# Last slice of a weight product in three rounded passes, row products moved into the attention, staged waits, new step orders

## What is computed

```
q, k, v = h @ Wq + bq, h @ Wk + bk, h @ Wv + bv
a = q @ k.T / sqrt(512);  a = a * adj + (1 - adj) * (-1e6)
x = x + softmax(a) @ v
h = relu(layernorm(x))
agg = segment_sum(h[src], dst) / max(degree, 1)
x = x + h + alpha * (agg @ W.T + b)
```

## Time and profile before

| what | value |
|---|---|
| runs | median 236.33 us, lowest 236.18, highest 236.58 (3 runs) |
| the profiled execution | 236.24 us, of which span 234.4 us |
| PE busy | 230.7 us, 98% of the span |
| DVE busy | 161.5 us, 69% |
| ACT busy | 82.0 us, 35% |
| POOL busy | 73.3 us, 31% |
| granted TensorE clock | full (2.4 GHz level) in all 40 slices |

### The profile page before, as it was taken

One profiled execution on the slowest core, in us unless ns is written; L12 is line 12 of the kernel. 1 busy time (PEld: TensorE's weight loads), 2 busy tenths in 40 slices (PEclk: granted clock), 3 DMA queues, 4 the chain that ended last, 5 costly groups with the idle time before them and its releaser, 6 DMA issues.

```text
span 234.4 us, 3310 instructions
## 1 busy us (share of the span) xinstructions
PE 230.7 (98%) x1290; PEld 188.6 (80%) x1290; DVE 161.5 (69%) x282; ACT 82.0 (35%) x151; POOL 73.3 (31%) x106
## 2 busy tenths in 40 slices
PE   8999999999999999999999999999999999999995
PEld 6475888888888888888888888888888888888884
DVE  5999999998889855884749975757574262073222
ACT  3598906773142330431452442424242002060000
POOL 4277024410000059950702570706064206000000
PEclk9999999999999999999999999999999999999999
DMA  6999102000000030050000000000000000001232
GB/s 198 336 391 402 66 0 49 0 0 3 0 3 0 6 86 3 3 179 0 0 0 3 0 0 0 3 0 1 0 0 3 0 0 0 3 3 45 108 115 90
DMA packets 7153, 12.30 MB, mean 52 GB/s; under 512 B 1121, under 2 KB 2145, under 8 KB 7009
## 3 DMA queue, kind: packets, MB, share of 16 engines
q1 hardware_dynamic: 6272, 11.67, 14.3%
q10 hardware_dynamic: 864, 0.40, 0.6%
HBM read 9.97 MB, written 2.10 MB: 52 GB/s over the span
## 4 chain that ended last, share of the span: by engine, by line
PE 98%; DVE 0%; issue 0%; POOL 0%; DVEq 0%; POOLq 0%
PE bank L821 22%; PE bank L823 22%; PE bank L822 22%; PE bank L970 12%; PE bank L842 8%; PE bank L899 3%; PE bank L990 3%; PE bank L892 3%; PE bank L876 2%; PE bank L816 1%; PE bank L886 1%; DVE o_sb L803 0%; PE bank L849 0%; PE bank L865 0%; POOL ones_r L355 0%
## 5 line engine op out<-in xcount | busy, mean ns | idle before, releaser
L446 ACT ACTIVATE h2f<-xs,nmr,rstd 128x512 f32<-128x512 f32 x8 | 6.5, 816 | 56.1 <-POOL nmr L385 56.1
L821 PE MATMUL bank<-V_hi,pT_hi 128*128 128x512 f32 x64 | 25.5, 399 | 0.0
L577 DVE TENSOR_TENSOR ohW<-iotaW,key_b 128x1280 bf16<-128x1280 bf16 (+4 forms) x33 | 25.1, 761 | 0.0
L821 PE MATMUL bank<-hT_hi,GT_hi 128*128 128x512 f32 x64 | 25.1, 392 | 0.0
L823 PE MATMUL bank<-hT_hi,GT_lo 128*128 128x512 f32 x64 | 25.0, 390 | 0.0
L822 PE MATMUL bank<-V_lo,pT_hi 128*128 128x512 f32 x64 | 24.9, 390 | 0.0
L823 PE MATMUL bank<-V_hi,pT_lo 128*128 128x512 f32 x64 | 24.9, 390 | 0.0
L822 PE MATMUL bank<-hT_lo,GT_hi 128*128 128x512 f32 x64 | 24.9, 389 | 0.0
L970 PE MATMUL bank<-A,h_hi 128*128 128x512 f32 x64 | 24.9, 389 | 0.0
L970 PE MATMUL bank<-A,h_lo 128*128 128x512 f32 x64 | 24.9, 389 | 0.0
L573 DVE TENSOR_TENSOR ohL<-iotaL,lo_b 128x1024 bf16<-128x1024 bf16 x33 | 22.5, 683 | 1.5 <-PE bank L842 1.4
(11 more groups left out here) (133 smaller groups left out, 519.6 us busy)
## 6 DMA issues: line engine op xcount, KB each, us to landing
xs<-in_x SPq DMA_DIRECT2D x4, 512.0 KB, 8.4
out_dram<-o_sb SPq DMA_DIRECT2D x7, 256.0 KB, 2.0
wv_raw<-in_wv SPq DMA_DIRECT2D x1, 1024.0 KB, 11.6
wk_rows<-in_wk SPq DMA_DIRECT2D x1, 1024.0 KB, 12.6
wq_rows<-in_wq SPq DMA_DIRECT2D x1, 1024.0 KB, 11.4
wt_raw<-in_wT SPq DMA_DIRECT2D x1, 1024.0 KB, 5.2
wq_raw<-in_wqT SPq DMA_DIRECT2D x3, 256.0 KB, 8.0
wk_raw<-in_wkT SPq DMA_DIRECT2D x3, 256.0 KB, 8.2
```

The lines of the kernel that those rows point to most:

```text
L577: nc.vector.tensor_tensor(ohW[:, q % RING, :, 0:row].rearrange("p b (m two) -> p b m two", two=2), bcast(iotaW[:, 0:row].rearrange("p (m t ...
L821: mm(out, lhs[0][a], rhs[0][b], start=(first and k == 0), stop=False)
```

## The change

1. The slice k = 3 of M, four float32 products before, becomes rounded parts: ACT writes `w_high` of both weights (steps mh0, mh1), DVE the rests `wq_low`, `wk_low` (ml0, ml1), and M0 to M3 are three float32r matmuls each. Slice k = 2 becomes a step Mk2 of its own, in float32.
2. The eight products with u leave the first part. In the attention ACT normalises each block once more into two buffers (rows_once_more), and DVE multiplies them there: blocks 0 and 1 after its last projection step, then two in each of the rounds i = 0, 1, 2, behind the row maximum and ahead of pT_lo. POOL makes negc for each block by two small instructions ahead of its fill. u_sb now lies where the edge keys were, so it is loaded only after the last one-hot batch, and on SP's queue behind the wait for G7. The adding of bv is spread: four blocks after the first two fills, then two each in i = 1 and i = 2.
3. A product of G or V is issued term by term (four hi·hi, four hi·lo, four lo·hi) and waits for each operand ahead of its own term. The load of the last weight no longer waits for all of add_bv.
4. All four orders are new; G7 is now the last projection instead of V7.

```diff
-PE_ORDER = ("Mk0 Mk1 c3 bb M0 c2 M1 c2 T0 M2 T1 M3 T2 T3 c3 G0 G1 G2 G3 c1 V0 T4 c3 V1 T5 c3 T6 V2 V3 T7 c3 V4 V5 c3 G4 G5 "
-           "G6 c3 V6 c2 G7 c2 V7 c3")
+PE_ORDER = ("Mk0 Mk1 bb c3 Mk2 c2 T0 M0 T1 c2 M1 c1 M2 M3 T2 T3 c2 G0 G1 G2 G3 c3 V0 T4 c2 V1 T5 c3 V2 V3 c2 T6 V4 c3 V5 T7 "
+           "V6 G4 c3 G5 G6 c2 V7 c2 G7 c3")
...
+        u_sb = place("u_sb", [P, D], F32, r_e + 2 * 4 * ET)
...
-            sp.dma_start(u_sb[:, :], u_d.partition_broadcast(P)).then_inc(u_back, 16)
-
             sp.wait_ge(proj, proj_index(("G", NT - 1)) + 1)
             sp.dma_start(bv_sb[:, :], bv_d.partition_broadcast(P)).then_inc(ld_bv, 16)
+            sp.wait_ge(oh_ready, NB)
+            sp.dma_start(u_sb[:, :], u_d.partition_broadcast(P)).then_inc(u_back, 16)
...
             sp.wait_ge(counts_final, 1)
-            sp.wait_ge(res_ready, NT)
...
+                pool.wait_ge(dots, i + 1)
+                link(nc.gpsimd.tensor_scalar(negc[:, i:i + 1], c_f[:, i:i + 1], bb[:, :], -1.0, ALU.add, ALU.mult))
+                link(nc.gpsimd.tensor_scalar(negc[:, i:i + 1], negc[:, i:i + 1], NEG, None, ALU.add))
...
-            for t in range(NT):
+            for t in range(4):
                 add_bv(t)
...
+                if i <= 2:
+                    add_bv(2 * i + 2)
+                    add_bv(2 * i + 3)
...
+                elif step == "mh":
+                    k = SPLIT + n // 2
+                    act.wait_ge((ld_wq, ld_wk)[n % 2][k], 16)
+                    nc.scalar.activation(w_high[:, k - SPLIT, n % 2, :], (wq_raw, wk_raw)[n % 2][:, k, :], ACT.Copy).then_inc(m_hi, 1)
...
+            def rows_once_more(t):
+
+                if t >= 2:
+                    act.wait_ge(dots, t - 1)
+                nc.scalar.activation(h2f[t % 2][:, :], xs[:, t, :], ACT.Relu, bias=nmr[:, 0, t:t + 1],
+                                     scale=rstd[:, 0, t:t + 1]).then_inc(renormed, 1)
...
+            def dot(t):
+
+                dve.wait_ge(renormed, t + 1)
+                nc.vector.tensor_tensor_reduce(
+                    out=h2f[t % 2][:, :], in0=h2f[t % 2][:, :], in1=u_sb[:, :], scale=1.0, scalar=0.0, op0=ALU.mult, op1=ALU.add,
+                    accum_out=c_f[:, t:t + 1]).then_inc(dots, 1)
+
+            dve.wait_ge(u_back, 16)
+            dot(0)
+            dot(1)
...
                     nc.vector.tensor_reduce(negmax[:, i:i + 1], pr[i % 2][:, :], AX.X, ALU.max, negate=True).then_inc(maxed, 1)
+                if i <= 2:
+                    dot(2 * i + 2)
+                    dot(2 * i + 3)
...
+                    mm(bank[2 + n][:, :], w_high[:, k, 0, block], w_high[:, k, 1, :], start=False, stop=False, skip_group_check=True)
+                    if n == 0:
+                        pe.wait_ge(m_lo, 2 * k + 2)
+                    mm(bank[2 + n][:, :], wq_low[:, KD - 1, block], w_high[:, k, 1, :], start=False, stop=False, skip_group_check=True)
+                    last = mm(bank[2 + n][:, :], w_high[:, k, 0, block], wk_low[:, KD - 1, :], start=False, stop=True,
+                              skip_group_check=True)
...
+                        term(ps[:, :], M[0], hT[0], blocks, first=True)
+                        if m == 0:
+                            pe.wait_ge(proj_lo, KD)
+                        term(ps[:, :], M[1], hT[0], blocks)
                         if m == 0:
                             pe.wait_ge(hT_lo, 4 * (half + 1))
-                            pe.wait_ge(proj_lo, KD)
-                        last = three_pass(ps[:, :], M, hT, [(cols(k, m), cols(k, half, HALF)) for k in range(KD)])
+                        last = term(ps[:, :], M[0], hT[1], blocks, final=True)
```

More of the change, by code:

```diff
@@ L164, in gnn_kernel @@
         wk_raw = place("wk_raw", [P, KD, D], F32, r_G + 8 * KB)
+        SPLIT = 3
+        w_high = place("w_high", [P, KD - SPLIT, 2, D], F32R, r_G)
+        wq_low = place("wq_low", [P, KD, D], F32R, r_G + 24 * KB)
+        wk_low = place("wk_low", [P, KD, D], F32R, r_G + 8 * KB)
         wk_rows = place("wk_rows", [P, KD, D], F32, r_V + 16 * KB)
@@ L177, in gnn_kernel @@
         R = place("R", [P, NT, N], I8, r_R)
-        u_sb = place("u_sb", [P, D], F32, r_R)
-        uh = [place(f"uh{i}", [P, D], F32, r_R + (2 + 4 * i) * KB) for i in range(2)]
+        u_scr = place("u_scr", [P, D], F32, r_R + 2 * KB)
         bk_row = place("bk_row", [P, D], F32, r_R + 6 * KB)
@@ L827, in three_pass, with term @@
                 return product(out, lhs, rhs, pairs, True, True)
+            def term(out, lhs, rhs, pairs, first=False, final=False):
+                for k, (a, b) in enumerate(pairs):
+                    last = mm(out, lhs[a], rhs[b], start=(first and k == 0), stop=(final and k == len(pairs) - 1))
+                return last
             def count(a, b):
```

85 lines of the change are left out of this document (52 added, 33 removed).

## The result

The changed kernel takes **236.9 us** (median of 18 runs, 235.98 to 238.23), the kernel before **236.35 us** (median of 18), a ratio of 1.0028 with a 95% interval of 1.0017 to 1.0038. The medians differ by +0.55 us; the ratio stands for +0.66 us, its interval for +0.4 to +0.9. So the change made the kernel slower by a little. The time lies inside the range of the prediction; whether it is beyond the 0.47 us that the prediction calls "the same" isn't certain. The profiled execution took 237.4 us, its span is 235.5 us (234.4 before).

A forecast was written before the change was run, and what follows sets the result against it. PE, busy 230.7 of 234.4 us, was taken as the bound. -0.45 us ahead of G0 plus 0.65 us in the attention gives +0.2 on 236.24, so 236.4, and with 0.09 for the median 236.5 us; range 235.4 to 238.3.

The forecast's parts named there:

- the same: Whole kernel: within 0.47 us of before; likeliest case, gain ahead of G0 mostly given back, 236.1 to 236.8, chance 0.40.
- PE's own work: PE up to the scores: float32r passes in M cut its work by about 0.6 us.
- G0 starts as if at 25.9 to 26.2: Ahead of G0: start there instead of 26.58, -0.4 to -0.7 us, less 0.1 later; -0.45 us taken.
- for a start at 25.8, no later than ACT does: At G0's third term: DVE's hT_lo, whole at 27.7, allows a G0 start at 25.8, no later than ACT.
- some tenths: In front of G0 in the kernel before: slack of some tenths of a us that staged waits could win.
- Nothing there makes PE wait by more than 0.1 us: From G0 to the scores: following the four orders finds no PE wait above 0.1 us.
- changes of kind: Behind G0, up to the scores: float32r matmuls behind another kind run longer, taking 0.1 us off the gain.
- The attention, +0.65: At the transposes of block 1: PE waits for pT_lo, 0.5 or 2.8 us; 0.65 us taken.
- slack: Ahead of block 1's transposes: undisturbed, pT_lo of block 0 comes at E + 17.1, wanted at 18.6, 1.4 us left.
- turns: DVE's products with u against POOL's instructions: 1.9 us lost where DVE keeps its turn, 4.3 us where they alternate.
- The scaling of b: Round 1 of the attention: products wait for POOL's last add_bv, scaling of b and third fill, about 0.6, or 0.6 + 1.2.
- the smaller loss: In the attention: the stall at block 1's transposes, 0.3 to 1.0 us in the likeliest case, chance 0.40.

The follow-up runs named there:

- float_slice: The changed kernel with slice 3 of the weight product in float32 again, without mh0, mh1, ml0, ml1; 237.07 us, ratio 1.0026 to the kernel before.
- after: The changed kernel as it is, in its first trace; 236.9 us, ratio 1.0028 to the kernel before.
- both_engines: both_again with mh0 later on ACT, one one-hot batch behind DVE's last hT_lo and its count behind G3; 237.8 us, ratio 1.0065.
- both repairs: The changed kernel with POOL's sum5, sum6 ahead of sq4 and DVE's products with u behind pT_lo; 236.2 us and, run again, 235.99 us.
- staged_only: The kernel before with only the term-by-term waits of G and V; 236.17 us, ratio 0.9992.
- dots_behind_pT: The changed kernel with DVE's products with u behind pT_lo instead of behind the row maximum; 236.26 us, ratio 1.0004 to the kernel before.
- no_pool_reads: The changed kernel with POOL writing zeros instead of adding bv to the residual; 236.26 us, ratio 1.0003 to the kernel before.
- both_mended: The changed kernel with sum5, sum6 ahead of sq4 on POOL and products with u behind pT_lo on DVE; 236.2 us, ratio 0.9999.
- u_first: The changed kernel with the load of u issued ahead of the wait for the last G and of bv's load; 236.87 us, ratio 1.0028.
- both_again: The kernel of both_mended run once more, on the chip of u_first; 235.99 us, ratio 0.9989 to the kernel before.
- after_again: The changed kernel once more, unchanged, for a second trace; 236.89 us, ratio 1.0018 to the kernel before.

## Why the prediction came out as it did

- **PE's own work**, forecast -0.6: the three passes save 0.5 us (float_slice against after). Right in kind and nearly in size.
- **"G0 starts as if at 25.9 to 26.2", -0.45.** G0 starts at 25.0 to 25.9 in the nine traces with the three passes (both_engines left out), but then waits inside, so only its end counts. Three measures of that end differ. By the first pair of traces it is -0.72 (36.87 instead of 37.59). Against S it is -0.2: 25.57 on the mean of ten traces with the changed order ahead of G, 25.79 in two of the kernel before; but S doesn't bind DVE (above). By the time of the two kernels with both repairs it is -0.2 to -0.4: they are 0.02 and 0.26 us faster than the kernel before by their ratios, and lose 0.18 behind G. So the gain is real in the traces, 0.2 to 0.4 is the best account of it, and -0.45 isn't excluded. The path was named in part: the prediction had DVE's last hT_lo at 27.7 and asked "for a start at 25.8, no later than ACT does"; the row says 27.63. It treated DVE and ACT as level and ACT as the one that may be late. DVE ends the wait in seven traces of nine, ACT in two. The slack of "some tenths" in the kernel before was 0.15 us (staged_only).
- **"Nothing there makes PE wait by more than 0.1 us"** from G0 to the scores. This is the step that failed, the largest error in the working. I followed the orders with the pitch that the norms had in the trace of before, where POOL's var_e took 0.34 us at this place; I didn't ask what stands behind it if DVE holds it off. It costs 0.8 to 0.86 us, in four of the six traces with the POOL order of the change. The two without it are of one chip, and there the medians show little of it too: dots_behind_pT and no_pool_reads lie 0.06 us above both_mended, where u_first lies 0.88 above both_again on another chip. Whether the chip decides isn't shown. Without the wait this stretch is 0.18 us longer than before (47.13 against 46.95); the prediction had 0.1 for changes of kind, and which part of the new orders costs it isn't shown.
- **The attention, +0.65.** End - E is 0.8, 0.5, 0.3 and 0.4 us above the kernel before in the four traces that have the products where the change puts them, and u late: 0.5 us on the mean. The mechanism was the one described: some slack, and a product that waits for a whole instruction of POOL. Three terms were off, in opposite directions. u_sb took 4.1 us to land in the first trace and 3.5 to 3.8 in the others with bv's load ahead of it, where I had 3.5, so the first product came at E + 4.2 to 4.7. The slack is 1.0 us, not 1.4 (u_first). And of the turns I had priced at 1.9 to 4.3 us in sum, one of 1.08 was taken ahead of block 1's transposes. The two engines did take turns: the first product began ahead of POOL's addition and lost nothing to it, the second waited for the whole of it. The scaling of b, for which I had counted 0.6, held up no product. (By its own terms 4.3 less 1.4 is 2.9, not 2.8.)
- **The range and the chances.** 236.9 lies in 235.4 to 238.3, a range of 2.9 us, made so wide by the turns that it says little for the mechanism. My likeliest case was "the same", 236.1 to 236.8; the median is 0.1 above its edge, and by the stall that this case names, 0.3 to 1.0 us, its edge should have been 236.9. I had the smaller loss named and the larger one not. That the two didn't push the time further up is luck: the traces add up to more than the medians show. Both repairs have the time at 236.2 and 235.99, and by the ratios below the two losses together cost 0.5 to 0.9 us, where the traces of after and after_again have 1.65 and 1.36. These two executions were slow ones of their kernel; how often each wait comes isn't known.
- **A faster version.** By their ratios to the kernel before, the changed kernel is at 1.0028 and 1.0018, the one with both repairs at 0.9989 (0.9975 to 1.0003) and 0.9999 (0.9988 to 1.001). So the repairs take 0.5 to 0.9 us off the changed kernel, and no run showed a version that beats the kernel before by more than the measurement can tell.

## What to carry to other kernels

Before work is taken off the engine that is 98% busy, ask of each stage which engine delivers its last operand: here the 0.5 us of TensorE work that went didn't move the end of G (float_slice), because VectorE, busy for all of 15.19 us ahead of it, delivered the last operand. In a fixed order, a short step that others wait for shouldn't stand behind a step that another engine can hold off: with the means ahead of the statistics none of five traces has the wait of 0.85 us. And compare single traces by distances between stages, but only from a point that the engine in charge really waits for.

## What the runs showed of the hardware that I had not expected

- A POOL instruction on 128x1 numbers took 2.86 to 3.37 us in four traces, with DVE running instructions with two inputs in SBUF back to back, and 0.32 or 0.38 us at the same place, beside the same instructions of DVE, in two others. In the long cases it ended with DVE's first accumulator read. The Trainium skill (page SBUF — State Buffer, section Who interferes with whom) says that issue order decides who blocks. The trace agrees that one engine waits for the other's whole instruction (1.77 us against 0.68 for a product), but here POOL was passed over at several ends of DVE instructions in a row. Why in some executions and not in others stays open.
- That section also has a DVE instruction with two inputs in SBUF contend with a GpSimd instruction that reads SBUF. POOL's addition of two tensors held up a product by 1.08 us; its scaling of b by one number per partition (101.23, 1.59 us long) overlapped two products that took 0.68 and 0.69 us, and took the same 1.6 us where no product ran beside it (no_pool_reads). Its fills of pr, which also read a tensor and one number per partition, did hold products up: 0.90 us instead of 0.68 at 108.93, with a fill from 108.15 to 109.28. What tells the two apart stays open.
- The start of the first count varied from 10.84 to 12.27 us between executions, more than any effect studied here.
